# A four-layer graph-attention kernel: attention columns of the weights made by TensorE, and another order of all operations in a turn

## What is computed

```python
h = relu(layernorm(x));  x = x + elu(softmax(mask(leaky(h@W@a1 + (h@W@a2).T))) @ h)   # layer 0
h = relu(layernorm(x));  x = x + gat2(gat1(h, W1), W2)   # layer 1: two GAT layers, 4 heads of 256, then 1 of 512
h = relu(layernorm(x));  x = x + softmax(mask(leaky(h@s + (h@t).T + b))) @ h          # layer 2
h = relu(layernorm(x));  x = x + relu(softmax(mask(leaky(scores(h@W_proj)))) @ (h@W_proj))   # layer 3, 8 heads

# one GAT layer of layer 1
xl = (x @ W).reshape(B, N, H, F)
asrc = einsum('bnhf,hf->bnh', xl, a_src); adst = einsum('bnhf,hf->bnh', xl, a_dst)
```

## Time and profile before

| | |
|---|---|
| median of 3 runs (lowest to highest) | 3154.17 us (3146.86 to 3154.77) |
| the profiled execution | 3162.35 us |
| its span, first to last instruction | 3160.6 us |
| PE busy | 2964.7 us, 94% |
| DVE, ACT, POOL busy | 80%, 74%, 72% |
| granted TensorE clock, mean | 0.974 of full |

### The profile page before, as it was taken

The page is one execution under the profiler, slowest core; times in us unless marked ns, Lnnn a source line. Parts: engine busy times, 40 slices in busy tenths (PEclk is TensorE's granted clock), DMA queues, the critical chain, the costliest instruction groups (busy, mean ns, idle before and its releaser), DMA issues. The chain is left out here.

```text
span 3160.6 us, 79056 instructions
## 1 busy us (share of the span) xinstructions
PE 2964.7 (94%) x20880; PEld 2695.9 (85%) x20880; DVE 2513.7 (80%) x8300; ACT 2343.1 (74%) x6433; POOL 2289.4 (72%) x3236
## 2 busy tenths in 40 slices
PE   1689999999999999999999999999999999999984
PEld 0678988988898898888888999899898999889974
DVE  5578888888887888888888888888888888788862
ACT  2467777777777777777777777777777777777753
POOL 4347777777777777777777787777777787777753
PEclk6899999999999999999999999999999999999985
DMA  4113333333333333333333333333333333333323
GB/s 131 43 52 113 110 120 113 120 117 107 120 117 117 116 111 122 111 117 116 109 120 114 117 116 113 120 111 121 113 120 116 107 123 114 118 115 111 115 97 105
DMA packets 204902, 352.53 MB, mean 112 GB/s; under 512 B 53296, under 2 KB 118960, under 8 KB 188080
## 3 DMA queue, kind: packets, MB, share of 16 engines
q1 hardware_dynamic: 204464, 347.49, 34.0%
HBM read 311.76 MB, written 35.59 MB: 110 GB/s over the span
## 5 line engine op out<-in xcount | busy, mean ns | idle before, releaser
L389 PE MATMUL bank_b<-w_hi,hT_hi 128*128 128x344 f32 x1536 | 468.6, 359 | 13.5 <-POOL w_lo L1399 8.8
L956 ACT ACTIVATE eT<-eT,tc 128x128 f32<-128x128 f32 x1024 | 314.0, 389 | 214.4 <-POOL eT L1493 214.4
L389 PE MATMUL bank_c<-w_hi,g_hi 128*128 128x258 f32 x2048 | 414.2, 284 | 5.7 <-DVE x L1170 5.6
L389 PE MATMUL bank_c<-w_lo,g_hi 128*128 128x258 f32 x2048 | 411.6, 283 | 0.0
L389 PE MATMUL bank_b<-w_lo,hT_hi 128*128 128x344 f32 x1536 | 410.2, 321 | 0.0
L1295 DVE CUSTOM_DVE_ANT_0 t_all_L<-t_all_L,mask 128x128 f32<-128x128 f32 x1024 | 385.1, 429 | 13.6 <-DMA t_all_L<-t_dram_L 13.5
L389 PE MATMUL bank_b<-w_hi,hT_lo 128*128 128x344 f32 x1536 | 357.9, 328 | 0.0
L389 PE MATMUL bank_c<-w_hi,g_lo 128*128 128x258 f32 x2048 | 350.0, 283 | 0.0
L389 PE MATMUL bank_e<-w_hi,hT_hi 128*128 128x264 f32 x1024 | 342.5, 350 | 3.0 <-DVE out_sb L1338 2.9
L389 PEld LDWEIGHTS bank_b<-w_hi,hT_hi 128*128 128x128 f32 x1536 | 278.6, 189 | 74.4 <-issue 64.8
L1410 POOL TENSOR_TENSOR rs<-rs,nhalf 128x1 f32<-128x1 f32 x512 | 309.7, 605 | 42.6
(11 more groups left out here) (138 smaller groups left out, 8647.1 us busy)
## 6 DMA issues: line engine op xcount, KB each, us to landing
shift_all<-shift_dram SPq DMA_DIRECT2D x128, 1024.0 KB, 7.1
t_all_L<-t_dram_L SPq DMA_DIRECT2D x128, 512.0 KB, 4.1
x_in<-in_x SPq DMA_DIRECT2D x128, 256.0 KB, 2.6
t_all_L1a<-t_dram_L1a SPq DMA_DIRECT2D x128, 256.0 KB, 3.2
out<-out_sb SPq DMA_DIRECT2D x128, 256.0 KB, 4.1
t_all_L<-t_dram_L SPq DMA_DIRECT2D x256, 64.0 KB, 3.4
adj_in<-in_adj SPq DMA_DIRECT2D x128, 64.0 KB, 2.5
t_dram_L1a<-t_rows_L1a SPq DMA_DIRECT2D x512, 0.5 KB
```

The lines of the kernel that those rows point to most:

```text
L389: last = mm(bank[:, 0:width], a[:, c * P:(c + 1) * P], w[:, c, b * width:(b + 1) * width], start=(first and c == chunks[0] and n == 0), st ...
L956: last = activation(eT[:, k, :], eT[:, k, :], ACT.Prelu, bias=tc3[:, k:k + 1], alpha=SLOPE)
```

## The change

**Weights.** The products with attention vectors leave DVE. The attention vectors come in arranged for the purpose (`in_att1`, `in_att2`, `in_att3`, arranged before the launch). PE transposes each block (`turn_weights`, 20 units of four 128x128 transposes), DVE copies the result to SBUF, and PE multiplies it with the attention vectors (`columns_of_weights`, four products with 2 or 4 columns). ACT and DVE split the small result. DVE also takes over part of the low parts: half of each W1 block and every other block of W2 and W_proj. There are six staging buffers in a longer list, and all 16 blocks are prepared before the turns begin. Whoever read `w_split` now waits for all 16 blocks (`chunk_ready`), and PE waits for them ahead of the first turn.

**Order.** All five lists of calls stand in another order. Most numbers in `t.graph(...)` are one lower. On PE this comes mostly from another place for the cut between two turns: four functions that stood at the end of the list now stand at its start, and what follows belongs to the graph one turn younger. Read around the circle, PE has three differences: `turn_mask` stands three places later, `product_L1a_first` stands ahead of `product_L1a_last`, and `product_L0` ahead of `product_L1b`. ACT, DVE, POOL and SP have more of them. `SKEW` is unchanged.

```diff
-            def split_weights(t):
-                for n in prepared.get(t.step, ()):
...
-                    for i in range(2):
-                        for head in range(count):
...
-                            last = nc.vector.tensor_tensor_reduce(
...
-                    last.then_inc(sem("ext_made"), 1)
...
+            def turn_weights(u):
+                n, q = units[u]
+                if q == 0:
+                    pe.wait_ge(sem(f"w_in{n % WR}"), 16 * (n // WR + 1))
+                for b in range(C):
+                    last = nc.tensor.transpose(turn_bank[u % 4][:, b * P:(b + 1) * P],
+                                               staged[n][:, q * D + b * P:q * D + (b + 1) * P], ident[:])
+                last.then_inc(sem("wt_turned"), 1)
...
+            def columns_of_weights(u):
...
+                pe.wait_ge(sem("wt_copied"), u + 1)
+                if q == 0 and n >= 2:
+                    pe.wait_ge(sem("w_lo_dve"), n - 1)
...
+            for u in range(len(units)):
+                turn_weights(u)
+                if units[u] == (2, 0):
+                    first_rows()
+                if u:
+                    columns_of_weights(u - 1)
+            columns_of_weights(len(units) - 1)
+            chunk_ready(pe, ALL - 1)
...
+            for n in range(ALL):
+                act.wait_ge(sem(f"w_in{n % WR}"), 16 * (n // WR + 1))
+                hi, _, src = w_parts(*w_chunks[n], n)[0]
+                activation(hi, src, ACT.Copy).then_inc(sem("w_hi"), 1)
+                if n:
+                    high_columns(n - 1)
+            high_columns(ALL - 1)
...
+            def low_parts(n):
+                (hi, lo, src), (e_hi, e_lo, e_src) = w_parts(*w_chunks[n], n)
+                dve.wait_ge(sem("w_hi"), n + 1)
+                if n < C:
+                    tt(lo[:, D:D1], src[:, D:D1], hi[:, D:D1].bitcast(F32), ALU.subtract)
+                elif n not in by_pool:
+                    tt(lo, src, hi.bitcast(F32), ALU.subtract)
+                dve.wait_ge(sem("w_hi_columns"), n + 1)
+                tt(e_lo, e_src, e_hi.bitcast(F32), ALU.subtract).then_inc(sem("w_lo_dve"), 1)
...
+            for u, (n, q) in enumerate(units):
+                dve.wait_ge(sem("wt_turned"), u + 1)
+                if u >= 4:
+                    dve.wait_ge(sem("wt_used"), u - 3)
+                nc.vector.tensor_copy(turned[u % 4], turn_bank[u % 4]).then_inc(sem("wt_copied"), 1)
+                if q == 0 and n:
+                    low_parts(n - 1)
...
             for step in range(G + SKEW):
                 t = Turn(G, step)
-                split_weights(t)
...
-                exp_L3_last(t.graph(10))
-                exp_L1a(t.graph(3))
-                leaky_L2(t.graph(6))
-                values_L3(t.graph(9))
...
+                exp_L1a(t.graph(3))
+                values_L3(t.graph(9))
+                exp_L3_last(t.graph(10))
```

434 lines of the change are left out of this document (219 added, 215 removed).

## The result

| | before | after |
|---|---|---|
| median of 7 runs each | 3155.65 us | 3133.25 us (3129.71 to 3138.51) |
| ratio, 95% interval | | 0.9929 (0.9917 to 0.9941) |
| the profiled execution, its span | 3162.35, 3160.6 us | 3129.71, 3127.9 us |
| granted clock, mean | 0.974 | 0.978 |
| the changed kernel once more, on another chip | 3160.75 us | 3141.6 us, ratio 0.9932 (0.9916 to 0.9947) |

The change is faster by 22 us, 0.7%. The forecast was 66.6 us. The direction was right, the time lies inside the range, and the forecast gain was three times too large.

What follows compares the result with a forecast made beforehand. PE was taken as the bound in the full turns, with waits of 0.52 us a turn. Gains of 50 us (turns), 16.6 (start) and 0 (end), 66.6 in all, from 3154.17 gave 3087.6 us; range 3055 to 3140.

Steps and rivals of the forecast that it cites:

- The waits of the turns: Full turns: PE's waits for xa, eB and p_L1b shrink to a few us in all; 50 us, 0.43 a turn.
- The slack of 0.9 us counted for xa: Full turns: the copy xa, which turn_h3 needs, comes 0.9 us earlier net, against a lateness of 0.2 to 0.7.
- What is late next: Full turns: pT_L0 just in time, DVE's residual with 0.3 us of slack; 10 of 60 us left as not won.
- The bound of 60 us: Full turns: the most an order can win, 0.52 us a turn over 115 turns.
- A turn in which little went wrong: Full turns: one turn of 22.64 us, set against the average of 23.16 us.
- The start: Before the full turns: first product of layer 1 at 72.7 instead of 89.36 us, 16.6 us gained and kept by later turns.
- the sum along DVE: Start: DVE's copies, low parts and layer 0 rows, 37 us, plus 10 of hand-overs; weights ready at about 47 us.
- the bound of 68: Start: weights ready at 68 us if PE stays at the half clock.
- The rule against the change: Start: DVE instructions with two SBUF inputs and POOL's SBUF reads delay each other; 8.5 to 19 us more.
- The end: Drain of layer 3's single graphs: order kept on each engine, so 0, plus or minus 5 us.
- the turns give nothing: Rival, full turns: other inputs are just as late as those now; 3138 us, chance 0.15.
- the start gives nothing: Rival, start: DVE and POOL block each other or clock at 1.2 GHz; weights at 61, 3102 us, chance 0.17.

Runs made afterwards that it cites:

- i_short_shift: The changed kernel with POOL's shift_L3_first on 16 of each 128 columns, the other columns of those heads left unshifted: 3068.38 us, ratio 0.9706 to the kernel before.
- g_spread_first: The changed kernel with one call moved on SP, spread_L1a ahead of send_L3: 3120.43 us, ratio 0.9873 to the kernel before.
- e_lows_on_pool: The changed kernel with all large low parts of the weights on POOL, none on DVE: 3149.08 us, ratio 0.9978 to the kernel before.

## Why the prediction was right or wrong

**The waits of the turns: right.** xa, eB and p_L1b went, as forecast, and the three gave 0.62 us a turn, more than the 0.43 counted on. Whether each of the reasons given (what moved ahead or behind on ACT and POOL) carried its part was not tried one by one. The slack of 0.9 us counted for xa held in the typical turn.

**"What is late next": the step that failed.** It looked at the places that the diff of PE's and ACT's lists points to, pT_L0 and the residual, and allowed 10 us for what would be late next. Neither shows up: the waits for them are 0 to 0.7 us. What was late next cost 0.47 us a turn, 54 us in 115 turns, and took back most of the 0.62. The lateness came from two engines that were only looked at as sources. On DVE the maxima moved beside another set of POOL's instructions, 4.28 us instead of 3.48, and `hT_lo_L3` ends 1.3 us later behind them; with one of the two long contentions gone, PE has the whole 0.47 back (`i_short_shift`). On SP the four issues of `send_L3` came in front of the spread of L1a; worth 19 us (`g_spread_first`). The text had the rule and the rows for the first loss and applied them to the start alone.

**The bound of 60 us: wrong.** "A turn in which little went wrong", 22.64 us, was taken as the floor. It was not even the shortest turn of that trace (22.48), and the least distances between PE's products add up to 22.2 to 22.4 us, depending on whether single odd ones count. Two kernels reached medians of 22.37 and 22.41. A shortest turn shows where one set of waits ends and bounds nothing.

**The start: the term mis-sized was PE.** Weights ready at 47 us was the sum along DVE, with PE at the full level (22 us for its groups); the bound of 68 was PE at half clock throughout. It was 57, and 60 in the second trace: half level to about 19 us, full to 33 (28 there), half behind that. With the clock held from 9.7 us on it was 49, and the first product of layer 1 came at 73.58, where the forecast said 72.7. So the sum comes out within 2 us where its condition holds (its terms were not checked one by one), and the clock was the step that failed: the full level was put into the sum without a reason. The only condition named for the half level was that PE has little to do, and here it fell on a full row. From ready weights to that product the trace took 24.5 us, the forecast 25.7. The first mark gained less than that product, 6.8 and 4.4 us against 8.1 and 5.3, so the start's gain was not kept whole by the later turns either.

**The rule against the change.** Its effect is there: of the six low parts of W2 and W_proj on DVE four took 1.01 to 1.04 us and one 1.48, beside 0.68 for the last; the four of W1 took 0.68 as well. That is 2.2 us more in all, where 8.5 to 19 were feared. It costs nothing here, because PE at the half clock was later anyway (`e_lows_on_pool`).

**The end:** 0 plus or minus 5 was forecast, 5.9 us less came in the profiled pair; the last products still wait 12.65 us for eT. What shortened it was not studied.

**The rivals.** By number the result, 3133, is nearest to "the turns give nothing" (3138), but not by mechanism: the start gave a quarter to two fifths of its term and the turns a fifth to two fifths of theirs. The mechanism of the start stood in another rival, "the start gives nothing": the clock at 1.2 GHz, weights ready at 61. Two terms fell short together, which the cases, each with one failure, did not hold. That the time still lies in the range is partly luck: the turns won more than forecast and gave back five times the 10 us allowed.

## What to carry to other kernels

When an order moves, list for every engine, the queues of DMA issues too, who takes each output and how late each may be, and not only the waits that the profile shows now: a shown wait that goes is replaced by the next, and here several stood within half a microsecond. Check which DVE instructions with two SBUF inputs fall beside long GpSimd ones, since the later of the two then lasts until the other's end. And don't read the shortest turn as a floor: add up the least distances of the bound engine instead, and take them from several kernels, since a wait that comes in every turn hides in the least distance of its own trace.

## What the runs showed of the hardware

**The clock fell on a full row.** PE was busy 5.00 of every 5 us from 10 to 55 us. Its work was fp32 transposes of 128x128 and products of 2 or 4 columns at the half level (2.45 us a unit), then from 15.4 us products of 512 columns, in which the level rose (granted clock 1.00 from 19.56 us), then the narrow work again, in which it fell: 1.00, 0.82, 0.50 (2.4 to 1.2 GHz) in the windows from 25 to 40 us. With four bf16 products of 256 columns in each unit of 1.7 us the clock, once at 1.00, stayed there until the row ended, in three traces. In two of them it also rose within these units (at 9.7 and 9.2 us), in the third it did not.

**A DVE instruction held by POOL ends with it.** A maximum of 128x128 with both inputs in SBUF takes 0.28 us; the 230 of a trace that started while one of two long POOL instructions ran ended 0.14 to 0.15 us behind it. Moving POOL's instruction changed which maximum is held and not the sum (4.28 and 4.27 us).

**SP's issues are held now and then.** In each trace 23 to 52 of some 2700 issues from 330 to 2960 us took over 0.5 us more than their median, `shift_dram<-shift_rows` being the most frequent, 19 to 47 us in all. Which issue it hits differs between kernels whose turns are the same, and what holds it stayed open.
